# An attention and FFN block on one core: rows of the schedule tables moved, and the split of the row maxima moved from POOL to VectorE

## The reference

```python
qkv = x @ c_attn_w + c_attn_b                       # x: 16 x 512 x 128
scores = einsum('bhqd,bhkd->bhqk', q, k) / sqrt(8)  # 16 heads, causal mask
attn = softmax(scores)                              # heads 0 to 2: a third of the keys scaled by 1.6, then normalised again
out = einsum('bhqk,bhkd->bhqd', attn, v) @ c_proj_w + c_proj_b
x = layernorm(x + out)
h = relu(s0 * [x, -x] @ W0) * 2                     # W = 1 where k is true, else -1
h = relu(s1 * h @ W1) * 2
x = layernorm(x + s2 * h @ W2)
```

## Time and profile before

| | |
|---|---|
| median of 3 runs | 973.31 us (972.83 to 976.41) |
| the profiled execution | 972.83 us |
| its span, from the first to the last instruction | 971.1 us |
| PE busy in the span | 831.8 us (86%) |
| DVE, POOL, ACT busy | 642.7, 581.0, 536.5 us |
| mean granted clock of TensorE | 0.948 of 2.4 GHz |

### The profile page before, as it was taken

How to read it: one execution, slowest core, us unless ns; L and a number is a source line. 1 busy time by engine, 2 the same in 40 slices (tenths; PEclk the granted TensorE clock), 3 DMA queues, 4 the chain that set the end, 5 groups by cost and what they waited for, 6 DMA issues and landing times.

```text
span 971.1 us, 17048 instructions
## 1 busy us (share of the span) xinstructions
PE 831.8 (86%) x5696; PEld 429.5 (44%) x5696; DVE 642.7 (66%) x2660; ACT 536.5 (55%) x946; POOL 581.0 (60%) x850
## 2 busy tenths in 40 slices
PE   3257779999999899999899899989899999999856
PEld 1113234545445454545444454545454454545333
DVE  3275757685857677685858677676858677774224
ACT  2105556665656666665656656665646666565712
POOL 1103336676675857676675858676665858475851
PEclk9557989999999999999999999999999999999977
DMA  3655534635353544534353544545343535300000
GB/s 75 63 65 77 59 65 48 70 44 75 43 77 42 73 54 64 69 46 73 43 78 41 73 49 73 61 46 79 44 73 43 72 37 72 52 19 6 23 0 22
DMA packets 66285, 53.17 MB, mean 55 GB/s; under 512 B 4534, under 2 KB 64150, under 8 KB 66198
## 3 DMA queue, kind: packets, MB, share of 16 engines
q1 hardware_dynamic: 65334, 51.30, 39.9%
q10 hardware_dynamic: 864, 0.79, 0.3%
HBM read 9.24 MB, written 4.19 MB: 14 GB/s over the span
## 4 chain that ended last, share of the span: by engine, by line
PE 42%; POOL 23%; DVE 16%; DMA 6%; issue 5%; ACT 4%; SPq 2%; ACTq 1%; POOLq 0%; DVEq 0%
DVE max_ps L690 7%; PE bank_ps L947 7%; PE max_ps L861 6%; POOL res L485 6%; PE bank_ps L948 6%; PE av_ps L920 6%; POOL h_lo L457 6%; PE score_ps L885 5%; POOL e L443 4%; PE bank_ps L993 3%; POOL rstd L477 3%; DMA stack<-rowmaxT 3%; DMA stack<-parts 2%; PE bank_ps L1005 2%; PE bank_ps L962 2%
## 5 line engine op out<-in xcount | busy, mean ns | idle before, releaser
L690 DVE CUSTOM_DVE_ANT_0 max_ps<-max_ps,future 128x512 f32<-128x512 f32 (+3 forms) x1024 | 477.8, 513 | 226.7 <-PE max_ps L861 224.3
L569 ACT ACTIVATE e<-score_ps 128x512 f32<-128x512 f32 x640 | 368.2, 598 | 324.2 <-PE score_ps L885 296.5
L885 PE MATMUL score_ps<-stack 75*128 75x512 bf16 (+3 forms) x1024 | 243.2, 301 | 40.8 <-DMA stack<-rowmaxT 18.7
L861 PE MATMUL max_ps<-stack 72*128 72x512 bf16 (+3 forms) x1024 | 247.0, 312 | 27.1 <-DMA stack<-parts 20.6
L443 POOL TENSOR_SCALAR_AFFINE_SELECT e<-e 128x512 f32<-128x512 f32 x256 | 160.4, 639 | 169.8 <-ACT e L569 169.7
L920 PE MATMUL av_ps<-e,vaug 128*25 128x512 f32 (+3 forms) x2048 | 190.0, 443 | 0.0
L457 POOL TENSOR_TENSOR h_lo<-full,h_hi 128x512 fp32r<-128x512 f32 x120 | 152.8, 1279 | 12.9 <-DVE h_hi L764 5.4
L861 PEld LDWEIGHTS max_ps<-stack 72*128 72x128 bf16 x1024 | 81.2, 99 | 166.4 <-issue 84.3
L885 PEld LDWEIGHTS score_ps<-stack 75*128 75x128 bf16 x1024 | 91.8, 98 | 115.2 <-ACT e L569 51.7
L690 DVE DVE_READ_ACCUMULATOR2_ANT rowmax<- 128x1 f32 x1024 | 140.4, 137 | 0.0
L561 ACT ACTIVATE full<-bank_ps,scales 128x512 f32<-128x512 f32 x128 | 87.8, 686 | 51.4 <-POOL h_lo L457 33.3
(11 more groups left out here) (86 smaller groups left out, 758.1 us busy)
## 6 DMA issues: line engine op xcount, KB each, us to landing
stack<-parts SPq DMA_DIRECT2D x288, 128.0 KB
x_in<-in_L_attn_hidden_states SPq DMA_DIRECT2D x16, 256.0 KB, 16.0
x_res<-in_L_attn_hidden_states SPq DMA_DIRECT2D x16, 256.0 KB, 3.3
out_x<-res SPq DMA_DIRECT2D x16, 256.0 KB, 3.6
stack<-rowmaxT ACTq DMA_DIRECT2D x32, 24.0 KB
e<-in_L_ffn_k SPq DMA_DIRECT2D x1, 256.0 KB, 3.3
e<-in_L_attn_c_attn_w SPq DMA_DIRECT2D x1, 128.0 KB
e<-in_L_ffn_k SPq DMA_DIRECT2D x1, 128.0 KB, 3.1
```

Source lines behind the costliest of these rows:

```text
L569: nc.scalar.activation(e[g % 2][:, t, :], score_ps[:, t % 2, :], ACT.Exp, scale=SCALE).then_inc(exped, 1)
L690: return nc.vector.tensor_tensor_reduce(out=scored_block, in0=scored_block, in1=future[:, P * (T - 1 - qt):S], scale=1.0, scalar=NEG, op0= ...
L861: return nc.tensor.matmul(out_ap[:, col:col + width], st[0:QK_ROWS, h, 0, P * qt:P * qt + P], st[0:QK_ROWS, h, 1, 0:width], start=True, st ...
L885: return nc.tensor.matmul(out_ap[:, col:col + width], st[0:ALL_ROWS, h, 1, P * kt:P * kt + P], st[0:ALL_ROWS, h, 0, P * kt:S], start=True, ...
```

## The change

Nothing of the computation changes; the tables are moved, `split_rowmax` is called on VectorE, one instruction at a time at the steps of NEGMAX_SPLIT, and the list of POOL is in another order.

```diff
-    ("tok_0", -1, (1, 1), (1, 1)),
+    ("tok_0", -1, (1, 0), (1, 0)),
...
-    ("attnT", -1, (1, 4), (1, 5)),
-    ("proj", -1, (1, 6), (1, 7)),
-    ("x1T", -1, (2, 5), (2, 5)),
+    ("attnT", -1, (1, 5), (1, 5)),
+    ("proj", -1, (1, 7), (1, 9)),
+    ("x1T", -1, (2, 6), (2, 6)),
...
-HIGH_STEPS = {"x1T": (2, 6), "ffn0_0": (2, 9), "ffn0_1": (3, 0), "ffn0_2": (3, 2), "ffn0_3": (3, 3),
+HIGH_STEPS = {"x1T": (2, 7), "ffn0_0": (2, 9), "ffn0_1": (3, 0), "ffn0_2": (3, 2), "ffn0_3": (3, 3),
...
-MIDDLE_STEP = (1, 0)
+MIDDLE_STEP = (0, 8)
+
+NEGMAX_SPLIT = (((3, 0), (3, 0), (3, 1), (3, 2)), ((0, 9), (1, 0), (1, 1), (1, 2)))
...
-LN_STATS = ((1, 8), (2, 1))
-LN_VAR = ((1, 9), (2, 2))
+LN_STATS = ((2, 1), (3, 5))
+LN_VAR = ((2, 2), (3, 6))
...
-SUMS_OUT = 8
+SUMS_OUT = 9
...
                 split_qk(0)
                 masks(0, 1)
-                rowmaxes(1)
+                split_qk(2)
                 masks(0, 2)
-                split_qk(2)
                 bias_residual()
                 masks(1, 0)
                 masks(1, 1)
+                layernorm_out(0)
                 masks(1, 2)
-                layernorm_out(0)
                 masks(2, 0)
-                layernorm_out(1)
+                low(0, 0)
+                low(0, 1)
                 masks(2, 1)
-                low(0, 0)
+                low(0, 2)
                 masks(2, 2)
-                rowmaxes(0)
-                low(0, 1)
-                low(0, 2)
                 low(0, 3)
                 masks(3, 0)
+                layernorm_out(1)
+                low(1, 0)
                 masks(3, 1)
-                low(1, 0)
                 masks(3, 2)
...
-                if t == 0 and g % 2 == 0 and b.c > 0:
-                    dve.wait_ge(rowmax_step, b.times(8, 4 * half - 4))
...
+            def split_rowmax(b, half, k):
+
+                m, r = rowmax[:, half], rowmax_rest[:, half]
+                hi, mid, lo = (rowmax_parts[:, half, :, i, :] for i in range(3))
+                if k:
+                    dve.wait_ge(rowmax_step, b.times(8, 4 * half + k))
+                else:
+                    dve.wait_ge(max_taken, b.times(G * STEPS, 2 * STEPS * (half + 1)))
...
+                        for k in range(4):
+                            if (g, t) == NEGMAX_SPLIT[0][k] and live(n + 1):
+                                split_rowmax(n + 1, 0, k)
+                            if (g, t) == NEGMAX_SPLIT[1][k] and live(n):
+                                split_rowmax(n, 1, k)
```

More of the change, by code:

```diff
@@ L458, in high_and_low_part @@
                                         ALU.subtract).then_inc(split_ready, 1)
-            def split_rowmax(b, half):
-                m, r = rowmax[:, half], rowmax_rest[:, half]
-                hi, mid, lo = (rowmax_parts[:, half, :, i, :] for i in range(3))
-                pool.wait_ge(max_taken, b.times(G * STEPS, 2 * STEPS * (half + 1)))
-                if b.c > 0:
-                    wait_full(pool, use_of(b + -1, f"rowmax{half}"))
-                nc.gpsimd.tensor_copy(hi, m).then_inc(rowmax_step, 1)
-                pool.wait_ge(rowmax_step, b.times(8, 4 * half + 1))
-                nc.gpsimd.tensor_tensor(r, m, hi, ALU.subtract).then_inc(rowmax_step, 1)
-                pool.wait_ge(rowmax_step, b.times(8, 4 * half + 2))
-                nc.gpsimd.tensor_copy(mid, r).then_inc(rowmax_step, 1)
-                pool.wait_ge(rowmax_step, b.times(8, 4 * half + 3))
-                nc.gpsimd.tensor_tensor(lo, r, mid, ALU.subtract).then_inc(rowmax_step, 1)
             def normalise_tokens(b, i):
@@ L514, in masks @@
                         mask(n, g, k)
-                def rowmaxes(half):
-                    b = n + (0 if half else 1)
-                    if live(b):
-                        split_rowmax(b, half)
                 low(1, 1)
```

9 lines of the change are left out of this document (added).

## The result

The changed kernel takes 1030.54 us (median of 4 runs, 1010.41 to 1039.56) against 973.52 us for the kernel before on the same chip: ratio 1.044, interval 1.032 to 1.057. It is slower, as forecast, but outside the range of 971 to 1009. Executions over 1.5% above the fastest of their kernel (1037.05 and 1039.56 us here, 1034.16 in the repetition) count as slow and are left out of every ratio, but not of the medians. Run again beside other kernels, the same file took 1013.34 us (1007.67 to 1034.16), ratio 1.039, interval 1.030 to 1.049. Its shortest executions (1007.67 and 1010.14 us) so stand at the upper edge of the range, and the executions spread more than those of before. The profiled execution took 1010.14 us (span 1008.4).

What follows compares the result with a forecast made beforehand. TensorE's own work plus waits in its queue bound the kernel. +0.1 + 0.9 + 0.1, about 1.1 us per iteration, times 14, plus about 1 for n = 15, gave 989; +3 for the clock made 992 us, range 971 to 1009.

Steps and rivals of the forecast that it cites:

- Step A: (0,8) to (1,7), token transposes earlier, avT copy later: 1.5 us wait added, projection's 1.00 us wait gone; net +0.1 us.
- Step B: Projection to first FFN layer: later residual addition makes res1 transposes wait 1.2 us instead of 0.43; +0.9 us.
- Step C: FFN's low parts: new 1.2 us wait for POOL's mask at (3,3), 1.06 us wait at (3,6) gone; sum +0.1 us.
- The second layernorm: zero: Statistics and normalisation of the second norm moved to (3,5), where VectorE and POOL have idle time: priced at zero.
- The row-max split moves from POOL to VectorE: Eight small instructions go to VectorE, at most 0.9 us per group, hidden by idle time or TensorE's wait: zero, at most 0.3 us.
- the wait at tok_0: Before the first token transposes, TensorE waits about 1.5 us for the later avT copy; taken to hide VectorE's second split group.
- The sign that was named for an error in the split's price: VectorE's maxima late for TensorE would show that the price of the row-max split was wrong.
- The clock: +3 us: Half-clock stretches of TensorE behind long waits, 1.4 us each: two or three in the whole run, +3 us, within 0 to 20.
- The rival "Clock": The four waits make a half-clock stretch in most iterations: 989 + 14 x 1.4 = 1009 us; chance 20%.
- Start and tail within 0.5: Outside the batch iterations, the run's start and tail were to change by no more than 0.5 us.

Runs made afterwards that it cites:

- best version: Kernel before with the second layernorm's statistics, variance and POOL part moved later and ScalarE's attnT copy one step earlier: 950.69 us, ratio 0.975.

## Why the prediction was right and where it was wrong

**The direction and the waits.** Step A: a wait of 1.3 to 1.6 us at the token transposes, none at the projection. Measured 1.29 and none. Step B: 1.0 to 1.4 at res1. Measured 1.16. Step C: 1.2 at the sums of (3,3), none at (3,6). Measured 1.12 and none. The sum of A, B and the gain of C without the mask is 54.10 + 0.1 + 0.9 - 1.06 = 54.04 us; the kernel with all parts but the split and POOL's new order has 54.01. Two signs were off: about 1 us was forecast before the first FFN matmul and 0.70 measured, and the iteration is 56.07 instead of 55.2.

**The second layernorm: zero.** Alone it brings 1.03 us per iteration: 0.81 at (3,6) and 0.23 before the first FFN layer. The first is step C's "in exchange the wait of 1.06 goes", which I had booked under the low parts; the mechanism was seen, but not that it could be had by itself, without the mask's wait. The best version rests on it.

**The failed step: "The row-max split moves from POOL to VectorE ... I take zero, upper bound 0.3 us."** It measured 1.19 us of TensorE's time in each of twelve iterations and 18.2 us over the run; with POOL's subtraction short the iteration gets 1.32 us back. Three things were wrong. The price: 225 ns came from a row where POOL stood still, so it was a lower bound and I used it as the upper one. The cover: I let the wait at tok_0 hide the split, but the first split instruction starts only as that wait ends (596.25 against 596.18), and the last one, which the transposes 4 us later need, stands behind three more, each queued behind a maximum. And the neighbours: I asked what VectorE does in that stretch, not what POOL does. The profile of before had the price on show. The same cast on VectorE, of an FFN result, in one iteration:

```profile
597.26 0.42 DVE L764 CAST h_hi<-full 128x512 fp32r<-128x512 f32 x1
...
600.45 0.75 DVE L764 CAST h_hi<-full 128x512 fp32r<-128x512 f32 x1 [2.10 <-ACT full L561]
```

The second began while POOL subtracted (598.42 to 600.92) and ended 0.28 us behind that. With the hold seen, the bounds would have been 0 to 2.1 us per instruction, the length of POOL's longest. 992 + 15 x 1.2 = 1010 us is the profiled execution's 1010.14, but that is partly luck: the steady iteration lost 1.97 us and not 1.1 + 1.2, and the ends of the run lost 14.7 us, of which the sum had about 4. The sign that was named for an error in the split's price, maxima late for TensorE, did not show either: these waits are 6.6 us over the run against 6.3 before. It was the split itself that was late.

The prediction did weigh the rule of the Trainium skill (GPSIMD Engine Reference, the table) that the two engines contend when VectorE has two SBUF inputs or a two-port mode, and applied it to one POOL norm only, where it held (3.14 us, from 610.88 to 614.02) and changed little. Another page of the Trainium skill (SBUF — State Buffer, section "Who interferes with whom") is sharper: the shared pair of ports is held for a whole instruction by whichever engine issued first, and the other "fully blocks", casts and copies from SBUF can take it, and a tensor_tensor contends with a GpSimd instruction that reads SBUF if both its inputs are in SBUF. By that rule each of the four split instructions is exposed and the row maximum is not. The trace agrees: 1.16, 1.94 and 2.16 us for instructions of 0.17 to 0.18, and 0.70 for the maximum beside a POOL subtraction.

**The clock: +3 us.** In the profiled execution it was near that: four of eleven steady iterations 0.6 us longer, which is less per stretch than the 1.4 us of the earlier trace rows. The spread between executions is another matter: 1007.67 to 1039.56 us of one file, with the median 20 us above the profiled execution. Spans of 1032.2 and 1034.5 us stood at a mean clock of 0.902 and 0.901, those of 1005.9 and 1008.4 at 0.940 and 0.938, which speaks for more time at half clock in the long ones; no trace of a long one was taken, so this is not shown. (Of two executions at 0.929 one has a span of 1013.0 and one of 1036.9 us. The means are not all comparable: in three of the traces here the record of the clock starts only 83 us into the span and lacks the first 60 us or so at half clock, which is worth 0.03.) I had priced the clock as one number instead of as a width of the range. The rival "Clock" (1009 us) was right to stand at the top, and should have been added to the sum with the split rather than stand in its place: it is no alternative to a new wait but comes on top of one.

**Ends of the run.** "Start and tail within 0.5" was wrong as well: 5.9 us before the first paired copy, 6.2 in the last three iterations. At the start a stretch at half clock of 17.1 us, and one of 3.4 in the first iteration, stand where the kernel before has one of 10.2. With POOL's subtraction short the first is 10.2 us and the first paired copy is at 139.5 us, as before. The last iterations lost 1.7, 3.2 and 1.3 us; each has 3.4 us at half clock, which none has before, and the middle one the wait of 2.2 us for the split; I have not separated these further.

**What stays open.** Why the same waits bring a half-clock stretch in each iteration of one kernel and in few of another. The changed kernel has waits of 1.29, 1.19, 1.16 and 1.12 us and four lengthened iterations of eleven; with POOL's order of before it has 1.29, 1.20, 1.15 and 0.70 and all of them are; the split alone with the early qk split has none. Behind waits of 1.85, 2.97 and 3.12 us it came in every steady iteration, but with 6.8, 27.3 and 13.7 us, so not in the order of the waits; and the split alone with the early qk split has a wait of 2.19 us in the iteration n = 15 with none behind it. No run here isolates it.

## What to carry to other kernels

Before moving a small instruction from GpSimd to VectorE, or beside it, list what GpSimd runs in the same microseconds: an SBUF-to-SBUF cast or two-input operation of 0.2 us can last until GpSimd's instruction ends, and everything queued behind it waits too. The price of a small instruction is to be taken from several rows of its kind, and a spread of durations for one shape (0.42 and 0.75) is a question to be answered before any sum. A step that moves several things at once is worth running apart: here one part alone was worth -1.5%, another +12%.

## What the runs showed of the hardware

- A single wait of 2.97 us on TensorE came with 27.3 us at the lower clock in each of twelve iterations of one execution, and the steady iteration grew by 10.75 us, over three times the wait. A wait of 3.12 us came with 13.7 us, one of 2.19 us once with none.
- Executions of the changed kernel differed by up to 3% (1007.67 to 1039.56 us); the kernel with the second layernorm alone and the best version, without a half-clock stretch in their steady iterations, repeat within 0.5% (956.63 to 959.60, 949.91 to 953.99).
